# Delta scan of a two-branch kernel: outputs from 32x32 tiles instead of block-diagonal 128x128 products

## What is computed

```python
def step(S, xs):
    qi, ki, ui, wi = xs
    attn = jnp.where(incl_lower, jnp.einsum('bhcd,bhmd->bhcm', qi, ki), 0.0)
    u_i = ui - wi @ S
    o_i = qi @ S + attn @ u_i
    S_new = S * lam_b + jnp.einsum('bhcd,bhcv->bhdv', ki, u_i)
    return (S_new, o_i)
```

## Time and profile before

| | us |
|---|---|
| median of 3 runs | 4021.34 |
| the profiled execution | 4022.32 |
| its span | 4020.5 |
| TensorE busy (matmul) | 3664.2 (91%) |
| VectorE busy | 3025.4 (75%) |
| ScalarE busy | 2876.9 (72%) |
| GpSimd busy | 2360.9 (59%) |
| mean granted clock of TensorE | 0.945 |

### The profile page before, as it was taken

How to read it: one execution, slowest core, us unless ns; L and a number is a source line. 1 busy time by engine, 2 the same in 40 slices (tenths; PEclk the granted TensorE clock), 3 DMA queues, 4 the chain that set the end, 5 groups by cost and what they waited for, 6 DMA issues and landing times.

```text
span 4020.5 us, 138077 instructions
## 1 busy us (share of the span) xinstructions
PE 3664.2 (91%) x57362; PEld 3021.4 (75%) x57362; DVE 3025.4 (75%) x5808; ACT 2876.9 (72%) x5487; POOL 2360.9 (59%) x2271
## 2 busy tenths in 40 slices
PE   4757654899999999999999999999999999999998
PEld 3746543688888888878888888888788888888886
DVE  4386675777788777787777877777877778777774
ACT  2423123688888888888888888888888888888886
POOL 1101111766666676766666767666666766676662
PEclk9777665999999999999999999999999999999999
DMA  2000000433333333334333333333343333343332
GB/s 63 23 29 1 12 12 9 117 96 92 91 90 97 106 90 93 92 92 120 92 92 90 86 102 106 92 92 92 88 115 92 92 87 92 103 112 96 100 93 57
DMA packets 149452, 331.77 MB, mean 83 GB/s; under 512 B 17632, under 2 KB 27616, under 8 KB 147168
## 3 DMA queue, kind: packets, MB, share of 16 engines
q1 hardware_dynamic: 148832, 322.93, 30.3%
HBM read 218.01 MB, written 104.86 MB: 80 GB/s over the span
## 4 chain that ended last, share of the span: by engine, by line
PE 66%; DVE 7%; ACT 6%; issue 4%; POOL 0%; DVEq 0%; ACTq 0%; POOLq 0%
PE bank L1697 19%; PE bank L1756 9%; PE bank L1814 8%; PE bank L1787 7%; PE bank L1734 7%; PE bank L1771 4%; PE bank L1864 3%; ACT L1355 3%; PE bank L1802 3%; PE bank L1855 3%; DVE rot_a L1497 2%; DVE rot_b L1504 2%; DVE ss L1512 2%; ACT pT L1289 1%; ACT gate L1355 1%
## 5 line engine op out<-in xcount | busy, mean ns | idle before, releaser
L1158 POOL TENSOR_TENSOR qk<-rot_a,rot_b 128x512 f32<-128x512 f32 x768 | 985.8, 1284 | 762.4 <-PE bank L1734 748.6
L1168 POOL TENSOR_TENSOR qk<-qk,rn 128x512 f32<-128x512 f32 x768 | 798.7, 1046 | 144.3 <-DVE rn L1576 144.3
L1497 DVE TENSOR_TENSOR rot_a<-bank,rot 128x512 f32<-128x512 f32 x768 | 529.3, 689 | 263.9 <-PE bank L1697 255.6
L1240 ACT ACTIVATE sq<-bank 128x512 f32<-128x512 f32 x768 | 461.4, 601 | 221.6 <-DVE rot_b L1504 164.7
L1697 PE MATMUL bank<-w_hi,xs_hi 128*128 128x512 f32 x1152 | 583.2, 506 | 34.9 <-POOL xs_lo L1148 18.5
L1512 DVE TENSOR_REDUCE ss<-sq 128x8 f32<-128x512 f32 x768 | 516.6, 673 | 46.3 <-ACT sq L1240 46.1
L1504 DVE TENSOR_TENSOR rot_b<-bank,rot 128x512 f32<-128x512 f32 x768 | 523.0, 681 | 0.0
L1734 PE MATMUL bank<-ident,qk 128*128 128x128 f32 x3072 | 470.6, 276 | 4.9 <-ACT qT L1251 2.9
L1697 PE MATMUL bank<-w_lo,xs_hi 128*128 128x512 f32 x1152 | 458.3, 398 | 0.0
L1697 PE MATMUL bank<-w_hi,xs_lo 128*128 128x512 f32 x1152 | 456.9, 397 | 0.0
L1756 PEld LDWEIGHTS bank<-kT,qT 64*32 64x32 f32 x24576 | 359.9, 107 | 120.5 <-issue 120.5
(11 more groups left out here) (238 smaller groups left out, 7113.2 us busy)
## 6 DMA issues: line engine op xcount, KB each, us to landing
vw<-value_scratch SPq DMA_DIRECT2D x576, 256.0 KB, 4.8
value_scratch<-v SPq DMA_DIRECT2D x192, 512.0 KB, 2.7
vw<-value_scratch SPq DMA_DIRECT2D x192, 192.0 KB, 3.8
stage<-in_wqkv SPq DMA_DIRECT2D x6, 1536.0 KB, 8.5
stage<-in_wb_all SPq DMA_DIRECT2D x6, 1088.0 KB, 9.8
stage<-in_band SPq DMA_DIRECT2D x6, 512.0 KB, 4.6
d_xt<-in_x SPq DMA_DIRECT2D x4, 512.0 KB, 3.8
base_scratch<-d_res SPq DMA_DIRECT2D x4, 512.0 KB, 3.3
```

The lines of the kernel that those rows point to most:

```text
L1158: nc.gpsimd.tensor_tensor(qk[:, c, :], rot_a[:, c % 2, :], rot_b[:, c % 2, :], ALU.add)\
L1168: nc.gpsimd.tensor_tensor(y, y, rn[:, x.q, 8 * c:8 * c + 8].unsqueeze(2).to_broadcast([P, 8, DH]), ALU.mult).then_inc(S["scaled"], 1)
L1240: nc.scalar.activation(sq[:, :], proj_bank(x, c)[:, :], ACT.Square).then_inc(S["squared"], 1)
L1497: nc.vector.tensor_tensor(rot_a[:, c % 2, :].rearrange("p (h d) -> p h d", h=8), proj_bank(x, c)[:, :].rearrange("p (h d) -> p h d", h=8), ...
```

## The change

The outputs are made like the recurrence, by 16 products of 32x32 for each of the two terms, directly from `state` and `ui`. `scanned` gets a part: part 0 (`q S`, not for `n = 0`) stands behind L878 of the same step, part 1 (`attn ui`) behind L889 of the same step. `blocks_uw(n + 4)` moves from behind L878 to the end of the step. Both parts of a chunk add up in PSUM; only the first product of each bank starts anew, and `skip_group_check` is set. The block-diagonal tiles, the copies into them, their memset and their three semaphores are gone, and with them the waits of VectorE and of `scanned`. ScalarE's four `u_out` and two squarings follow one another.

```diff
@@ gpsimd, group
-                need(pool, S["var_steps"], g * 9)
-                nc.gpsimd.memset(sqr[:, NB:3 * NB, :], 0.0).then_inc(S["diag_zero"], 1)
-                pool.wait_ge(S["diag_zero"], g + 1)
-                for n in range(L // C):
-                    pool.wait_ge(S["ui"], g * 8 + n + 1)
-                    if n >= 2:
-                        pool.wait_ge(S["od"], g * 8 + n - 1)
-                    for h in range(H):
-                        r = slice(h * D, (h + 1) * D)
-                        nc.gpsimd.tensor_copy(ui_diag[r, n % 2, :, r], ui[r, n % 2, :, :]).then_inc(S["ui_diag"], 1)
@@ scalar, group
-                act.wait_ge(S["diag_zero"], g + 1)
-                for n in range(1, L // C):
-                    act.wait_ge(S["scan_s"], g * 8 + n)
...
-                    for h in range(H):
-                        r = slice(h * D, (h + 1) * D)
-                        nc.scalar.activation(state_diag[r, n % 2, :, r], state[r, n % 2, :, :], ACT.Copy)\
-                            .then_inc(S["state_diag"], 1)
...
+                u_out(2)
+                u_out(3)
+                square_centred(3, 0)
+                square_centred(0, 1)
@@ vector, scan
-                    if n >= 2:
-                        dve.wait_ge(S["ui_diag"], g * 32 + 4 * (n - 1))
...
-                    if n >= 2:
-                        dve.wait_ge(S["state_diag"], g * 28 + 4 * (n - 1))
@@ tensor, group
-                def scanned(n):
-
-                    pe.wait_ge(S["ui_diag"], g * 32 + 4 * (n + 1))
-                    if n > 0:
-                        pe.wait_ge(S["state_diag"], g * 28 + 4 * n)
+                def scanned(n, part):
+
                     for b in range(GS):
-                        out = ps[:, 1 + n // 4 * 2, b * P + n % 4 * C:b * P + (n % 4 + 1) * C]
-                        if n > 0:
-                            T.matmul(out, state_diag[:, n % 2, b, :], qc[:, (b * 8 + n) * C:(b * 8 + n + 1) * C], start=True, stop=False)
-                        mm = T.matmul(out, ui_diag[:, n % 2, b, :], atT[:, b * 8 + n, :], start=n == 0, stop=True)
-                    mm.then_inc(S["od"], 1)
+                        for h in range(H):
+                            r = slice(h * D, (h + 1) * D)
+                            out = ps[r, 1 + n // 4 * 2, b * P + n % 4 * C:b * P + (n % 4 + 1) * C]
+                            if part == 0 and n > 0:
+                                T.matmul(out, state[r, n % 2, b, :], qc[r, (b * 8 + n) * C:(b * 8 + n + 1) * C],
+                                         start=n == 4 and b == 0, stop=False, skip_group_check=True)
+                            if part == 1:
+                                mm = T.matmul(out, ui[r, n % 2, b, :], atT[r, b * 8 + n, :], start=n == 0 and b == 0, stop=True,
+                                              skip_group_check=True)
+                    if part == 1:
+                        mm.then_inc(S["od"], 1)
...
-                    if n < 4:
-                        blocks_uw(n + 4)
-                    if n > 0:
-                        scanned(n - 1)
+                    scanned(n, 0)
                     pe.wait_ge(S["ui"], g * 8 + n + 1)
...
                     mm.then_inc(S["sd"], 1)
-                scanned(L // C - 1)
+                    scanned(n, 1)
+                    if n < 4:
+                        blocks_uw(n + 4)
```

More of the change, by code:

```diff
@@ L206, in delta_mixer @@
         cen = sb("d_cen", [P, 4 * NB, D])
-        diag = sqr[:, NB:3 * NB, :].rearrange("p n d -> p (n d)").rearrange("p (k v b c) -> p k v b c", k=2, v=2, b=GS)
-        state_diag, ui_diag = diag[:, 0, :, :, :], diag[:, 1, :, :, :]
         taps = cen[:, 0:3 * CONV * P // D, :].rearrange("p b d -> p (b d)").rearrange("p (a k c) -> p a k c", a=3, k=CONV)
@@ L236, in delta_mixer @@
             "n2_steps", "unit_t", "unit_c", "vkb", "kk", "na", "na_u", "inv_init", "inv_steps", "tT",
-            "pe_blocks", "at_out", "uw", "uu_out", "w_out", "diag_zero", "state_diag", "ui_diag", "s_zero", "ws", "ui", "sd", "od", "scan_s", "short_steps",
+            "pe_blocks", "at_out", "uw", "uu_out", "w_out", "s_zero", "ws", "ui", "sd", "od", "scan_s", "short_steps",
             "streams", "ssum", "mean_steps", "var_steps", "cen", "v_first", "v_first_silu", "v_first_turned", "vtok",
@@ L404, in group @@
                 u_out(1)
-                act.wait_ge(S["diag_zero"], g + 1)
-                for n in range(1, L // C):
-                    act.wait_ge(S["scan_s"], g * 8 + n)
-                    if n >= 2:
-                        need(act, S["od"], g * 8 + n - 1)
-                    for h in range(H):
-                        r = slice(h * D, (h + 1) * D)
-                        nc.scalar.activation(state_diag[r, n % 2, :, r], state[r, n % 2, :, :], ACT.Copy)\
-                            .then_inc(S["state_diag"], 1)
[L414 to L421, removed]
+                u_out(2)
+                u_out(3)
+                square_centred(3, 0)
+                square_centred(0, 1)
                 if not last:
```

## The result

| | before | after |
|---|---|---|
| median of the runs, us | 4021.3 (4020.25 to 4021.45, 4 runs) | 3968.62 (3966.87 to 3969.75, 4 runs) |
| the profiled execution, us | 4022.32 | 3966.87 |
| its span, us | 4020.5 | 3965.1 |
| mean granted clock of TensorE | 0.945 | 0.951 |

The ratio is 0.9867 (95% interval 0.9855 to 0.9879): 52.7 us, 1.3% faster. The forecast was 3976 us; the time lies in the range and in the forecast case.

What follows compares the result with a forecast made beforehand. TensorE's output products bound the old scan, its instruction supply the new: 7.5 intervals of 3.9 us plus the ends give 32.2 us instead of 43.4, 45 us saved in four scans, so 3976 us; range 3950 to 3994.

Steps and rivals of the forecast that it cites:

- forecast case: Instruction supply limits the four new scans: 32.2 us each instead of 43.4, 3976 us in all; chance 80%.
- The bound: TensorE's output products bound the old scan; the new one outruns the instruction supply, with about 11 more packets.
- The size of the interval: Time between TensorE restarts in the new scans: 3.9 us per 128 records, read from the first group's stops.
- The other terms of the scan: Beside the interval's size: 7.5 intervals a scan, plus 1.4 us before the first boundary and 1.2 and 0.3 at the end.
- The price of 32 small records: Time of 32 records of 32x32 products on TensorE, taken from L878: 0.58 us.
- The steps: Supply-bound steps of the new scan: late ones 3.9 us, early ones (n < 4) about 4.9 us.
- Rival A: The instruction supply keeps up in the scans: 22.4 us each, 84 us saved, 3937 us; chance 12%.
- Rival B: Packets come slower in a row; at 5.9 us an interval 4036 us. Chance 5% slower, 3% no difference.
- The copies at nothing: Removing 128 GpSimd and 112 ScalarE copies and four memsets from the scans gives nothing.
- The place of the products: Part 0 fills TensorE's wait for `ui` (0.7 to 1.2 us after L878's start); part 1 runs beside VectorE's state update.
- what follows: Work behind each scan moves up, so 45 us reach the end; projections may meet stops up to 2 us in three groups.

Runs made afterwards that it cites:

- 3: Changed kernel with every product of part 1 issued twice, 1344 records a scan and false outputs: 3997.61 us, ratio 0.9932.
- 6: The bfloat16 kernel of 5 with every output product issued twice, 1088 records a scan and false outputs: 3973.4 us, ratio 0.9876.
- 4: Changed kernel without its output products but for four of part 1 a step, 672 records a scan: 3930.01 us, ratio 0.9763.
- 5: Changed kernel with the outputs' operands in bfloat16, copied by GpSimd and ScalarE, 848 records a scan: 3944.53 us, ratio 0.9806.
- 2: Changed kernel with both output parts of the chunk before put between `w S` and `k ui`, `blocks_uw` back behind `w S`: 3974.37 us, ratio 0.9876.
- 1: Kernel before with its block-diagonal output products moved behind `k ui`, copies and 128x128 products kept: 4012.72 us, ratio 0.9974.
- 7: Changed kernel with 64 waits for a long-reached semaphore on TensorE behind `k ui` in each step: 4037.93 us, ratio 1.0038.
- 8: Kernel before with the same 64 waits behind `k ui` in each step: 4104.48 us, ratio 1.0203.

## Why the prediction was right

- **The bound.** Right. The scan went from TensorE's products to the supply of its instructions: 33 stops in four scans, 128 records apart, one packet each, and 11 more packets, as forecast. 3 and 6 add records and move the time by 29.0 and 28.9 us, where their products' own work was priced at 11 and 4; 4 and 5 take records away, and in their first scans TensorE idles 2.2 and 5.0 us with "issue" instead of 10.0.
- **The size of the interval.** This is the term that was mis-sized. The prediction took 3.9 us from the first group's stops and added 7.5 of them to 2.9 us: 32.2 us a scan. The mean of 29 intervals was 3.60, and 7.5 x 3.60 + 2.9 is 29.9; measured were 29.8. Four scans give 9.6 us more, against the 7.4 by which the time fell short of 3976. The value was outside the rows that the prediction had, which began at 3.69 and which it read as growing. In the second group of the changed kernel it was as low as 3.46 in the mean, in the fourth single ones reached 4.15. The step that was off is taking the interval of the earlier trace rows as that of the scan. In the rows from 152.13 to 163.90 the packet starts 1.62 us behind a restart and TensorE restarts 2.3 us behind that; in the changed scans it is 1.17 and 2.44. So the shortfall lies ahead of the packet, and 2, with 1.46 there, has the forecast's 3.9. Why this delay differs is open: no other queue carried anything beside the packets in the stretch shown.
- **The other terms of the scan** were each off and cancel, which is luck. The forecast had 7.5 intervals and 2.9 us at the two ends. Measured are 8, 7, 7 and 7, 7.25 in the mean, and 3.7 us at the ends, since in the third and fourth scan TensorE runs 3.66 and 3.91 us from the first `ui` before a stop ends (and in the first such a restart comes before it). 7.25 x 3.60 + 3.7 is again 29.8.
- **The price of 32 small records**, 0.58 us, was read where a 128x128 product follows. Between small products it is 0.42 to 0.45 us in the changed kernel (177.28 to 177.70, 178.43 to 178.88). It moved nothing, since the supply bounds the scan.
- **The steps.** Late ones of 3.9 us were forecast and are 3.5 to 4.0 in the first group. The early ones came out shorter than the 4.9 forecast: from the second to the fifth `ui` of the first group (163.12 to 175.67) they take 4.2 us, and 4.3 in the mean of the four groups (3.9 to 5.4).
- **Rival A**, the supply keeps up, 22.4 us a scan. Fallen for this kernel. Its price can't be checked: 4, which asks for little supply, has a first scan of 21.8 us and reaches 3930 where A said 3937, but it lacks the output products that A's price holds and still has a few stops. The 38.6 us between 4 and the changed kernel are what the supply and the outputs' own work take together. A agrees with scans that hold products of 128x128: in the first scan of 1 (160 to 200 us) and the fourth of the kernel before (580 to 623 us), TensorE has no wait that ends with "issue". In the changed kernel, with tiles alone, it has nine from 157 to 192 us, 10.0 us together.
- **Rival B**, the packets come slower in a row. Fallen: eight or nine in a row came at 3.60 us in the mean, below the first four intervals of the kernel before.
- **The copies at nothing.** In line with the runs, not isolated. In the kernel before, no wait of VectorE in the first scan ends with a copy, and TensorE's waits there (160 to 205 us) end with VectorE or "issue" alone, but for its weight load, 0.17 us each at 164.68 and 175.28. 5 and 6 put 15 copies a group back beside the scan, and 6 is 4.8 us above the changed kernel; 1 keeps all the old ones and gains what its order gives. GpSimd is 52.6 us and ScalarE 34.9 us less busy on the page. That the first is so near the gain of 52.7 us is chance, since next to nothing waited for GpSimd (weight loads of TensorE, 1.2 us in the four scans together).
- **The place of the products.** The prediction argued part of its chain from it (`ui` ready while part 0 runs). With the supply as the bound it is worth 4 to 8 us (2, by ratios, medians or scans), at least in part through a longer interval, and without the small tiles 11.5 (1).
- **The clock and what follows.** The forecast has no term for the clock. The granted clock (1 is full speed) was 0.55 in the first scan's stretch after (157 to 192 us, TensorE busy 24.20 of 35.00 us) and 0.53 in the earlier trace rows, at 38.04 busy us of 43.00. No run here shows what sets it. The three stretches behind a scan are 2.0 us shorter together, where up to 2 us each were feared lost.

## What to carry to other kernels

Count instructions before splitting a product into small ones: here 16 float32 products of 32x32 are 64 instructions for 0.45 to 0.58 us of work, and TensorE got 256 of them every 3.6 to 3.9 us. Up to that rate small tiles should win, by the author's estimate from the prices of a late step: 0.9 to 1.16 us for the 64 small records of the outputs, against 3.55 us for the 16 of 128x128. No run here has the full outputs below that rate by tiles of float32 alone. Above it a further record cost 25 to 32 ns, and fewer instructions are what helped (bfloat16 in 5, 24.1 us below the changed kernel); a larger tile that the data fill was not run. The sign is a stop that ends with "issue", at one spacing, in step with the packets of the instruction queue; the spacing should be taken as a mean over many of them, in the stages that the change makes dense, and it can shift by 0.3 us with the order of the same products (2).

## What the runs showed of the hardware

- One 16 KB packet of the instruction queue is 256 of TensorE's instructions (8 packets for 2048 in 3, 4 for 1024 in 7 and 8). In dense small work one came every 3.60 us in the mean in the changed kernel (3.4 to 4.2 in single cases), 3.69 in 6, 3.73 in 3 and 3.89 in 2, though the work between two stops took only some 2.3 us in the changed kernel's late steps.
- In these scans one packet at a time was under way. It started 1.17 us behind a restart in the mean in the changed kernel, 1.46 in 2, and the next restart came 2.44 us behind its start in both.
- A float32 product of 32x32 leaves two matmul records, a bfloat16 one leaves one (32 against 16 in 5). With the number of records put back to 1088 (6) the type brought nothing: 3973.4 us against 3968.6.
- Two waits in a row for a semaphore that has long come were put into one instruction, and it took TensorE some 97 ns (7 and 8), as much as six small records; 80 ns of it reached the time in 8.
- 32 records of 32x32 by 32 columns took 0.42 to 0.45 us until the next small product started, at a granted clock of 0.50 (177 to 188 us of the changed kernel), and 0.58 us until a 128x128 one did (1).
